# A four-layer cross-attention and feed-forward kernel: its first norm and query split made batch by batch, with queries moved to ScalarE's queue and selectors to GpSimd

## The chip, the core and the metric

The kernel runs on one core of a Trainium2 chip. The core has five engines, which run side by side and meet only at semaphores: TensorE (PE, matrix products), VectorE (DVE), ScalarE (ACT), GpSimd (POOL) and SyncE (SP), which here only issues DMA transfers. The metric is the device time of one execution in microseconds (us); lower is better.

## What is computed

The input `x` holds 2 batches of 256 tokens of width 128. Four layers follow, each a cross-attention or self-attention and a feed-forward block, each behind a norm. The change touches only the first attention, layer 0: 16 heads of width 8, queries from the normalised `x`, keys and values both the raw context of 2 batches of 512 tokens.

```python
def _layernorm(x, axis=-1, eps=1e-05):
    m = jnp.mean(x, axis=axis, keepdims=True)
    v = jnp.var(x, axis=axis, keepdims=True)
    return (x - m) / jnp.sqrt(v + eps)
...
        energy = jnp.einsum('nqhd,nkhd->nhqk', q, k)
        attn = jax.nn.softmax(energy / jnp.sqrt(jnp.float32(EMBED_SIZE)), axis=3)
        out = jnp.einsum('nhql,nlhd->nqhd', attn, v).reshape(N, q_len, EMBED_SIZE)
        return out @ w_out.T + b_out
...
    x = x + _L0_xattn_ref(ctx_1024, ctx_1024, _layernorm(x, axis=-1), L0_xattn_w_out, L0_xattn_b_out)
    x = x + _L0_ffn_ref(_layernorm(x, axis=-1), ...)
```

## The kernel before

The program is written engine by engine, with semaphores by hand; each engine works its own list in order, and an instruction that waits holds everything behind it on that engine. A DMA issue is an instruction of the engine whose queue it uses; before the change all of them are SyncE's.

**The first attention.** Scores are made in bf16, with each fp32 value split into three bf16 parts (`split_rows`, five VectorE steps: part 0, the rest, part 1, the rest, part 2). The parts of keys and queries lie with all heads in the partitions; the score products want one head's parts in rows. So they go through DRAM: `store_keys` and `store_queries` write the parts to `Kscr` and `Qscr`, `load_keys` and `load_queries` read them back into `Kst` and `Qst`, four heads per load, three loads per four heads. Rows 0 to 11 of `Kst` are *selectors*: ones that pick the right head's maximum out of rows 0 to 11 of `Qst`, where the split negative maximum of each query is written later. Before the change ScalarE writes all eight selector tiles (12x2048, four heads each).

**Groups and steps.** The 2 batches of 16 heads make 8 groups `g` of four heads; groups 0 to 3 are batch 0. `attention_cross(0)` runs in steps of 8 slots. In step `s`, TensorE makes the 8 maximum blocks of group `s` (`max_block`, L1761, one 128x512 product each, in two banks turn by turn, so that a block waits for the reduction two before it), and VectorE reduces each (`max_bank`, L993). GpSimd splits the group's maxima into three parts (`split_max`, L503 to L507), TensorE turns them in slot 4 of the next step (`turn_max`, L1818), and ScalarE copies them into `Qst` (L646). In step `s` TensorE also makes the scores of group `s - 2` (L1743), and the products of the exponentials with the values of group `s - 3` (L1845), which read `Vaug`, a copy of the context (L489, GpSimd). In the first three steps `max_block` is followed by busywork products (L1772), whose results nobody reads; `keep_busy` (L2060) is the same ahead of the attention.

**The opening, in the order of each list.** SyncE loads `x`, half of the turned context, the constants, the other half; then stores keys and queries of batch 0, with their loads mixed; then the context (`CTXN`), keys and queries of batch 1, and the weights. VectorE: statistics of all four tiles of `x`, the key split of batch 0, the norm of all four tiles, the query split of batch 0 (out of PSUM, after TensorE has turned the norm), the key and query splits of batch 1, the addition of the bias row `bo0` to `x`, and then the attention. GpSimd: the power of the variance (`rstd_of`), three casts, the wait for `CTXN` and its copy into `Vaug`, four memsets, and then `split_max` for all groups.

## Time and profile before

| | before |
|---|---|
| median of 3 runs | 552.3 us (551.53 to 555.41) |
| the profiled execution's own time | 551.78 us |
| its span, first to last instruction | 549.9 us |
| TensorE busy | 491.1 us (89%) |
| VectorE busy | 354.1 us (64%) |
| ScalarE busy | 309.8 us (56%) |
| GpSimd busy | 72.7 us (13%) |
| mean granted TensorE clock | 0.972 of full |

The span is one profiled execution. Busy times of different engines overlap, so they don't add up to it. An engine that is less than wholly busy is not free in every stretch; which engine sets the pace has to be read stretch by stretch. Products on TensorE are pipelined, so the duration of one contains its way through the array: the distance from one start to the next is what it costs in a row of them.

### The profile page before, as it was taken

Reading aid. Unit: us, or ns where it says so; the run is one execution under the profiler, and the core shown is the slowest. Engines: PE = TensorE matmul, PEld = TensorE weight load, DVE = VectorE, ACT = ScalarE, POOL = GpSimd, SP = SyncE. Lnnn points to the kernel's source line nnn. Section 1 sums busy time; section 2 is a strip of 40 time slices with the busy share of each in tenths; the row PEclk is TensorE's granted clock in tenths of the full one; section 3 lists DMA queues with packets and bytes.
Section 4 is the critical chain, followed back from the end, with each engine's and each line's share of the span. In section 5 each row is a group of like instructions: output and inputs, shape, how many; then the busy total and the mean of one; then the engine's idle time right before and its main releaser. Section 6 shows DMA issues by size and latency. Waiting matters only on the chain.

```text
span 549.9 us, 9205 instructions
## 1 busy us (share of the span) xinstructions
PE 491.1 (89%) x3320; PEld 302.8 (55%) x3324; DVE 354.1 (64%) x912; ACT 309.8 (56%) x530; POOL 72.7 (13%) x186
## 2 busy tenths in 40 slices
PE   5869998999989998798978599999999967898997
PEld 2224455998954444443734235555655655556987
DVE  5848755766689773398335647787698457545664
ACT  6428787463425779137366369888577404554331
POOL 4021111100011110000082000000042312000000
PEclk9979999999999999999999899999999977999999
DMA  4669401014425000000000000000000050000000
GB/s 144 189 167 400 166 2 36 1 30 131 123 63 176 3 0 2 1 1 0 2 0 0 2 0 0 1 2 1 2 1 2 15 217 0 1 1 2 2 10 11
DMA packets 11612, 26.17 MB, mean 48 GB/s; under 512 B 2128, under 2 KB 6864, under 8 KB 10928
## 3 DMA queue, kind: packets, MB, share of 16 engines
q1 hardware_dynamic: 11568, 25.59, 14.1%
q8 instruction: 27, 0.44, 0.4%
q14 instruction: 17, 0.14, 0.1%
HBM read 22.44 MB, written 3.15 MB: 47 GB/s over the span
## 4 chain that ended last, share of the span: by engine, by line
PE 71%; DVE 14%; issue 5%; ACT 5%; SPq 2%; DMA 2%; POOL 1%; DVEq 0%; ACTq 0%; POOLq 0%
PE ps L2091 5%; PE ps L2079 5%; PE ps L1761 5%; PE ps L1967 5%; PE ps L1978 5%; PE ps L1845 5%; PE ps L1993 5%; PE ps L1933 4%; PE ps L1743 4%; DVE mxs L993 3%; PE ps L2050 2%; PE ps L1945 2%; PE ps L1860 1%; PE ps L1772 1%; PE ps L2037 1%
## 5 line engine op out<-in xcount | busy, mean ns | idle before, releaser
L634 ACT ACTIVATE PR<-ps 128x1024 f32<-128x1024 f32 x80 | 77.4, 977 | 42.1 <-PE ps L1719 18.4
L993 DVE TENSOR_REDUCE mxs<-ps 128x1 f32<-128x512 f32 x128 | 81.7, 682 | 24.8 <-PE ps L1761 23.4
L1114 DVE TENSOR_REDUCE nm<-ps 128x1 f32<-128x512 f32 x64 | 41.1, 683 | 22.1 <-PE ps L1967 21.7
L1761 PE MATMUL ps<-Kst,Qst 84*128 84x512 bf16 x128 | 49.6, 394 | 6.2 <-DVE mxs L993 3.8
L678 ACT COPY PR<-ps 128x512 f32<-128x512 f32 x64 | 37.9, 595 | 21.9 <-PE ps L1978 21.9
L686 ACT ACTIVATE Qst<-ps,nm 128x512 f32<-128x512 f32 x64 | 45.5, 711 | 2.7 <-DVE nm L1114 2.7
L1743 PE MATMUL ps<-Qst,Kst 84*128 84x256 bf16 x256 | 46.1, 274 | 0.1
L468 POOL TENSOR_SCALAR ve<-mv 128x2 f32<-128x2 f32 (+1 forms) x13 | 3.0, 233 | 306.5 <-DVE mv L1171 169.3
L1978 PEld LDWEIGHTS ps<-const_t,Qst 128*128 128x128 f32 x256 | 27.5, 140 | 26.6 <-DVE Qst L1094 14.4
L717 ACT ACTIVATE PR<-ps,cols_t 128x256 f32<-128x256 f32 x64 | 26.5, 471 | 23.4 <-PE ps L2079 23.0
L1978 PE MATMUL ps<-const_t,Qst 128*128 128x128 f32 x256 | 35.4, 280 | 3.0 <-DVE Qst L1094 2.0
L1967 PE MATMUL ps<-VX,FC 64*128 64x512 f32 x128 | 36.1, 641 | 0.1
L1845 PE MATMUL ps<-PR,VX 128*9 128x256 f32 x512 | 33.5, 380 | 0.0
L646 ACT COPY Qst<-ps 12x1024 bf16<-12x1024 bf16 x20 | 20.0, 999 | 23.6 <-PE ps L1818 23.6
L1743 PEld LDWEIGHTS ps<-Qst,Kst 84*128 84x128 bf16 x256 | 23.5, 98 | 15.1 <-issue 3.4
L2091 PEld LDWEIGHTS ps<-FC,PR 128*128 128x128 f32 x256 | 30.9, 192 | 0.8
L1094 DVE TENSOR_SCALAR Qst<-Qst,rsum 128x512 f32<-128x512 f32 x64 | 30.6, 520 | 1.1
L2079 PE MATMUL ps<-parts,FC 128*128 128x256 f32 x128 | 30.4, 380 | 0.9 <-DVE scr L1054 0.8
L1993 PE MATMUL ps<-PR,Kst 128*64 128x256 f32 x256 | 31.2, 385 | 0.0
L1933 PE MATMUL ps<-scr,FC 128*128 128x256 f32 x128 | 30.6, 382 | 0.6 <-DVE scr L1054 0.6
L2091 PE MATMUL ps<-FC,PR 128*128 128x128 f32 x256 | 31.0, 275 | 0.0
L1761 PEld LDWEIGHTS ps<-Kst,Qst 84*128 84x128 bf16 x128 | 12.4, 98 | 32.9 <-DVE mxs L993 23.4
(389 smaller groups left out, 894.6 us busy)
## 6 DMA issues: line engine op xcount, KB each, us to landing
Kst<-k_rows SPq DMA_DIRECT2D x48, 96.0 KB
FC<-in_fc SPq DMA_DIRECT2D x2, 2048.0 KB, 12.2
Qst<-q_rows SPq DMA_DIRECT2D x48, 48.0 KB
FC<-in_w SPq DMA_DIRECT2D x1, 2048.0 KB, 7.4
k_rows<-REP SPq DMA_DIRECT2D x12, 128.0 KB, 2.2
REP<-in_w SPq DMA_DIRECT2D x1, 1536.0 KB, 7.2
q_rows<-REP SPq DMA_DIRECT2D x20, 64.0 KB, 2.0
FC<-in_w2e SPq DMA_DIRECT2D x1, 1024.0 KB, 9.4
```

The lines of the kernel that those rows point to most:

```text
L634: act.activation(PRg[:, g % 2, u * 1024:u * 1024 + width], bank(3 + 2 * (n % 2), 2)[:, 0:width], ACT.Exp, scale=scale).then_inc(s.p_ready, 1)
L686: act.activation(P3[:, i % 8, :], bank(S_BANKS[n % 2][half]), ACT.Exp, bias=nm3[:, i % 8:i % 8 + 1], accum_out=sum3[:, i % 16:i % 16 + 1]) ...
L993: i = dve.tensor_reduce(m[:, u // 4, u % 4:u % 4 + 1], bank(n % 2), AX_X, ALU.max)
L1743: i = pe.matmul(bank(3 + 2 * (n % 2), 2)[:, k * SQ:(k + 1) * SQ], Kst[0:ROWS_A, b, h0 + u, k * P:(k + 1) * P], Qst[0:ROWS_A, b, h0 + u, :] ...
L1761: pe.matmul(bank(n % 2), Qst[0:ROWS_A, b, h, q0:q0 + P], Kst[0:ROWS_A, b, h, :], start=True, stop=True).then_inc(s.smax_ready, 1)
L1845: i = pe.matmul(o[32 * c:32 * c + HD + 1, :], Vaug[:, 4 * b + k, h0 + c, 0:HD + 1], pr[:, c * 1024 + k * SQ:c * 1024 + (k + 1) * SQ], star ...
L1933: i = pe.matmul(bank(2 * (n % 2) + c // 2)[:, c % 2 * SQ:(c % 2 + 1) * SQ], w13[:, e, c * P:(c + 1) * P], lnT[:, b * SQ:(b + 1) * SQ], sta ...
L1967: pe.matmul(bank(S_BANKS[n % 2][half]), Q3[d0:d0 + DH3, r, q0:q0 + P], K3[d0:d0 + DH3, r, b * SK:(b + 1) * SK], start=True, stop=True)\
L1978: ins = pe.transpose(bank(T_BANKS[half])[:, k * P:(k + 1) * P], P3[:, i % 8, k * P:(k + 1) * P], ident)
L1993: pv = pe.matmul(bank(o3_bank(g))[DH3 * c:DH3 * (c + 1), r * SQ:(r + 1) * SQ], V3[:, 4 * b + k, DH3 * (h0 + 2 * r + c):DH3 * (h0 + 2 * r + ...
L2079: i = pe.matmul(bank(2 * (n % 2) + c // 2)[:, c % 2 * SQ:(c % 2 + 1) * SQ], fc1[:, n % E, c * P:(c + 1) * P], hdT[:, n % 3, :], start=True ...
L2091: i = pe.matmul(bank(4 + n % 2)[:, j * P:(j + 1) * P], actT[:, n % 2, c, j * P:(j + 1) * P], fc2[:, n % E, c, :], start=(c == 0), stop=(c ...
```

## The change

Five edits, all in the opening and in the first attention:

1. `x` is loaded in two halves, and statistics, power, norm and turn of norm 0 are done for each batch by itself. On VectorE the norm of batch 0 stands between the key split's second and third step; the statistics and norm of batch 1 follow after the queries of batch 0. TensorE's first two busywork products are gone and the eight behind become seven.
2. Batch 0's queries are stored and loaded from ScalarE's list, with batch 0's selectors between; SyncE issues all key loads of batch 0 without the queries between them.
3. Batch 1's four selectors are written by GpSimd, ahead of `split_max`.
4. GpSimd splits the maxima of groups 0 and 1 before it waits for the context and copies it. `CTXN` lies in another buffer (`scr` instead of `PR`). ScalarE no longer waits for that copy before the attention.
5. Batch 1's turned queries are copied by ScalarE from bank 7 to `lnT`, and VectorE splits them inside step 2, after its first reduction. The bias row `bo0` is added inside step 3.

```diff
-        CTXN = PR[:, 0:1024].rearrange("p (k n) -> p k n", k=KT)
+        CTXN = scr[:, T:3 * T].rearrange("p (k n) -> p k n", k=KT)
...
-            sp.dma_start(x[:, :, :], d["x"]).then_inc(s.ld_x, 16)
+            sp.dma_start(x[:, 0:2, :], d["x"][:, 0:2, :]).then_inc(s.ld_x, 16)
...
+            sp.dma_start(x[:, 2:4, :], d["x"][:, 2:4, :]).then_inc(s.ld_x1, 16)
             sp.dma_start(ctxT[:, SK:NK], d["ctxT"][:, SK:NK]).then_inc(s.ld_ctxT1, 16)
             store_keys(0, 0)
-            load_keys(0, 0, 0, 1)
-            store_queries(0, 0)
-            load_keys(0, 0, 1, 2)
-            load_queries(0, 0, 0, 2)
-            load_keys(0, 0, 2, 4)
-            load_queries(0, 0, 2, 4)
+            load_keys(0, 0, 0, 4)
             sp.dma_start(onesel[:, :, :], d["onesel"]).then_inc(s.ld_onesel, 16)
             sp.dma_start(CTXN, d["ctx"]).then_inc(s.ld_ctx, 16)
             store_keys(0, 1)
-            store_queries(0, 1)
+            store_queries(sp, 0, 1)
             load_keys(0, 1)
-            load_queries(0, 1)
+            load_queries(sp, 0, 1)
...
-            rstd_of(0)
+            for b in range(B):
+                rstd_of(0, b, of_batch(b))
...
-            pool.wait_ge(s.ld_ctx, 16)
-            pool.tensor_copy(Vaug[:, :, :, 0:HD], CTXN.rearrange("p k (h c) -> p k h c", h=H))\
-                .then_inc(s.setup_pool, 1)
-            link(pool.memset(onebv[:, :], 0.0))
-            for part in range(NPART):
-                link(pool.memset(onebv[32 * part:32 * part + 1, :], 1.0))
-            def split_max(a):
-
-                for g in range(G):
+            for q in range(4):
+                pool.tensor_copy(Kst[0:MAXR, 1, 4 * q:4 * q + 4, :],
+                                 C["selrow"][0:MAXR, 4 * q:4 * q + 4].unsqueeze(2).to_broadcast([MAXR, 4, SK]))\
+                    .then_inc(s.sel_ready1, 1)
+
+            def split_max(a, g0=0, g1=G):
+
+                for g in range(g0, g1):
...
-            split_max(0)
+            split_max(0, 0, 2)
+            pool.wait_ge(s.ld_ctx, 16)
+            pool.tensor_copy(Vaug[:, :, :, 0:HD], CTXN.rearrange("p k (h c) -> p k h c", h=H))\
+                .then_inc(s.setup_pool, 1)
+            split_max(0, 2, G)
+            link(pool.memset(onebv[:, :], 0.0))
...
-            for b in range(B):
-                for q in range(4):
-                    act.copy(Kst[0:MAXR, b, 4 * q:4 * q + 4, :],
-                             C["selrow"][0:MAXR, 4 * q:4 * q + 4].unsqueeze(2).to_broadcast([MAXR, 4, SK]))\
-                        .then_inc(s.sel_ready, 1)
-            act.wait_ge(s.setup_pool, 3)
...
+            select(0, 0)
+            select(0, 1)
+            store_queries(act, 0, 0)
+            load_queries(act, 0, 0, 0, 2)
+            select(0, 2)
+            load_queries(act, 0, 0, 2, 4)
+            select(0, 3)
+            act.wait_ge(s.xn_turned, 2)
+            act.copy(lnT[:, 0:SQ], bank(7)[:, 0:SQ]).then_inc(s.q0_copied, 1)
             attention(0)
...
+                        if a == 0 and step == 2 and part == 0:
+                            dve.wait_ge(s.q0_copied, 1)
+                            split_rows(Qparts[:, :, SQ:T], lnT[:, 0:SQ], rest[:, 0:SQ], None, 'q_split')
+                        if a == 0 and step == 3 and part == 0:
+                            add_row(C["bo0"])
...
+            turn_rows(0, 0, bank(0))
             pe.wait_ge(s.ld_ctxT, 16)
-            keep_busy(2, 7)
...
-            keep_busy(8, 6)
+            keep_busy(7, 6)
+            turn_rows(0, 1, bank(7))
```

How the lists change at the three places that matter here. In each row stands the source line, the operation, what it writes and reads, the size, and the semaphores for which it waits. SyncE before, from the keys of batch 0 to its last query load but one piece (L377 loads keys, L385 stores queries, L393 loads them):

```order
L377 DMA Kst<-k_rows 24x2048 [waits k_stored0]
L377 DMA Kst<-k_rows 24x2048 x2
L385 DMA q_rows<-REP 16x8x256 [waits q_split]
L385 DMA q_rows<-REP 16x8x256
L385 DMA q_rows<-REP 16x8x256 [waits q_split]
L385 DMA q_rows<-REP 16x8x256
L385 DMA q_rows<-REP 16x8x256 [waits q_split]
L377 DMA Kst<-k_rows 24x2048 [waits k_stored0]
L377 DMA Kst<-k_rows 24x2048 x2
L393 DMA Qst<-q_rows 24x1024 [waits q_stored0]
L393 DMA Qst<-q_rows 24x1024 x5
L377 DMA Kst<-k_rows 24x2048 [waits k_stored0]
```

ScalarE after, from its first selector to the attention (L707 selectors, L367 stores, L375 loads, L719 the copy of batch 1's queries):

```order
L707 CAST Kst<-const_t 12x2048 [waits ld_const]
L707 CAST Kst<-const_t 12x2048
L367 DMA q_rows<-REP 16x8x256 [waits q_split]
L367 DMA q_rows<-REP 16x8x256
L367 DMA q_rows<-REP 16x8x256 [waits q_split]
L367 DMA q_rows<-REP 16x8x256
L367 DMA q_rows<-REP 16x8x256 [waits q_split]
L375 DMA Qst<-q_rows 24x1024 [waits q_stored0]
L375 DMA Qst<-q_rows 24x1024 x5
L707 CAST Kst<-const_t 12x2048
L375 DMA Qst<-q_rows 24x1024 [waits q_stored0]
```

The stores and loads of batch 0's queries have left SyncE's list and stand in ScalarE's, between its selectors.

GpSimd before, from its power to the first split of maxima:

```order
L469 TENSOR_TENSOR rstd<-ve,nhalf 128x4 [waits pool_done]
L485 CAST identb<-const_t 128x128 [waits ld_const]
L486 CAST maskb<-const_t 128x128
L487 CAST maskb<-const_t 128x128
L489 COPY VX<-PR 128x128x8 [waits ld_ctx]
L491 MEMSET onebv 96x128
L493 MEMSET onebv 1x128 [waits pool_done] x3
L503 TENSOR_SCALAR mp<-mxs 128x2x4 [waits smax_read,pool_done]
```

And after (`VX` holds `Vaug`; L499 begins a group's split):

```order
L464 TENSOR_SCALAR ve<-mv 128x2 [waits var_ready]
L465 TENSOR_TENSOR rstd<-ve,nhalf 128x2 [waits pool_done]
L482 CAST identb<-const_t 128x128 [waits ld_const]
L483 CAST maskb<-const_t 128x128
L484 CAST maskb<-const_t 128x128
L486 CAST Kst<-const_t 12x2048 x4
L499 TENSOR_SCALAR mp<-mxs 128x2x4 [waits smax_read]
```

The wait for the context (`ld_ctx`) no longer stands ahead of the first split; four selectors and a second power do.

VectorE before, at the end of its opening:

```order
L970 CAST REP<-ps 128x256 [waits xn_turned,k_split]
L966 TENSOR_TENSOR rest<-ps,REP 128x256 [waits q_split]
L974 CAST REP<-rest 128x256 [waits dve_done]
L975 TENSOR_TENSOR rest<-rest,REP 128x256 [waits q_split]
L976 CAST REP<-rest 128x256 [waits dve_done]
L1138 TENSOR_TENSOR x<-x,const_t 128x512 [waits q_split]
L993 TENSOR_REDUCE mxs<-ps 128x1 [waits smax_ready,dve_done]
L993 TENSOR_REDUCE mxs<-ps 128x1 [waits smax_ready] x15
L993 TENSOR_REDUCE mxs<-ps 128x1 [waits smax_ready,m_ready]
```

And after, from the first reductions to step 3:

```order
L1005 TENSOR_REDUCE mxs<-ps 128x1 [waits smax_ready] x16
L1005 TENSOR_REDUCE mxs<-ps 128x1 [waits smax_ready,m_ready]
L982 CAST REP<-scr 128x256 [waits q0_copied]
L978 TENSOR_TENSOR rest<-scr,REP 128x256 [waits q_split]
L986 CAST REP<-rest 128x256 [waits dve_done]
L987 TENSOR_TENSOR rest<-rest,REP 128x256 [waits q_split]
L988 CAST REP<-rest 128x256 [waits dve_done]
L1005 TENSOR_REDUCE mxs<-ps 128x1 [waits smax_ready,q_split]
L1005 TENSOR_REDUCE mxs<-ps 128x1 [waits smax_ready] x6
L1005 TENSOR_REDUCE mxs<-ps 128x1 [waits smax_ready,m_ready]
L1155 TENSOR_TENSOR x<-x,const_t 128x512
```

The second batch's query split and the bias row have moved behind 17 and 25 reductions.

## Rows read from the trace of the kernel before

**Rows 1.** The page: the span, and busy time of TensorE

```profile
span 549.9 us, 9205 instructions
PE 491.1 (89%) x3320; PEld 302.8 (55%) x3324; DVE 354.1 (64%) x912; ACT 309.8 (56%) x530; POOL 72.7 (13%) x186
```

**Rows 2.** The chain that ended last, 26 to 44: start us, us, what

```profile
23.25 5.24 DMA PR<-in_ctx
28.55 1.04 POOL VX L489
...
30.58 0.27 POOL mp L503
...
32.10 0.38 PE ps L1818 x2
```

**Rows 3.** TensorE's timeline: start us, busy us, line, operation, tiles, shapes, count

```profile
5.76 3.78 PE L2060 MATMUL ps<-ctxT,const_t 128*128 128x512 f32 x4 [5.76 <-DMA const_t<-in_const]
...
10.19 7.47 PE L2060 MATMUL ps<-ctxT,const_t 128*128 128x512 f32 x16
18.71 0.59 PE L1761 MATMUL ps<-Kst,Qst 84*128 84x512 bf16 x2 [1.05 <-DMA Qst<-q_rows]
...
26.70 0.38 PE L1761 MATMUL ps<-Kst,Qst 84*128 84x512 bf16 x1
...
42.82 0.38 PE L1761 MATMUL ps<-Kst,Qst 84*128 84x512 bf16 x1
...
49.62 0.39 PE L1761 MATMUL ps<-Kst,Qst 84*128 84x512 bf16 x1
```

**Rows 4.** Stretches: us, busy of PE, PEld, DVE, ACT, POOL; PEclk; DMA; GB/s

```profile
27.00:32.10 5.10, 0.08 (x1) 0.00 (x0) 0.69 (x1) 0.00 (x0) 2.90 (x10) 0.95 0.58 172
32.10:38.30 6.20, 6.20 (x17) 2.34 (x18) 3.22 (x5) 1.00 (x1) 1.10 (x5) 0.50 0.75 186
```

**Rows 5.** SyncE's timeline, its DMA issues: key loads, query stores, query loads

```profile
10.93 3.10 SPq L385 DMA_DIRECT2D q_rows<-REP  x5
...
15.49 2.41 SPq L393 DMA_DIRECT2D Qst<-q_rows  x6
...
29.58 4.80 SPq L377 DMA_DIRECT2D Kst<-k_rows  x12
```

**Rows 6.** ScalarE's timeline: the eight selectors

```profile
5.74 14.48 ACT L704 CAST Kst<-const_t 12x2048 bf16<-12x2048 f32 x8 [3.53 <-DMA const_t<-in_const]
```

**Rows 7.** VectorE's timeline: keys' first step, norm, query split, bias row

```profile
4.70 0.39 DVE L970 CAST REP<-ctxT 128x512 bf16<-128x512 f32 x1
...
7.50 1.20 DVE L878 TENSOR_SCALAR xn<-x,mv,rstd 128x128 f32<-128x128 f32 x4
10.43 0.42 DVE L970 CAST REP<-ps 128x256 bf16<-128x256 f32 x1 [1.74 <-PE ps L2067]
...
12.14 0.29 DVE L976 CAST REP<-rest 128x256 bf16<-128x256 f32 x1
...
17.33 0.69 DVE L1138 TENSOR_TENSOR x<-x,const_t 128x512 f32<-128x512 f32 x1
```

**Rows 8.** Query stores (L385), whole span: from issue to landing

```profile
DMA to landing us min/median/max: 1.9/2.0/2.6
```

**Rows 9.** GpSimd's groups by shape: busy us, mean ns of one, idle before

```profile
L469 POOL TENSOR_TENSOR rstd<-ve,nhalf 128x2 f32<-128x2 f32 x8 | 5.8, 720 | 0.7
...
L489 POOL COPY VX<-PR 128x1024 f32<-128x1024 f32 x1 | 1.0, 1042 | 20.7 <-DMA PR<-in_ctx 20.7
...
L546 POOL CAST parts<-rest 128x320 bf16<-128x320 f32 x1 | 0.5, 526 | 0.1
L486 POOL CAST maskb<-const_t 128x128 bf16<-128x128 f32 x1 | 0.5, 513 | 0.0
...
L544 POOL CAST parts<-rest 128x320 bf16<-128x320 f32 x1 | 0.5, 451 | 0.1
...
L487 POOL CAST maskb<-const_t 128x128 bf16<-128x128 f32 x1 | 0.3, 293 | 0.0
```

More of the change, by code:

```diff
@@ L278, in mega_kernel @@
         NUNIT = B * E
-        NORMS = [(0, 0), (1, 0), (2, 0), (1, 1), (2, 1), (3, 0), (3, 1)] + [(k, 0) for k in range(4, 8)] + \
+        NORMS = [(0, 0), (0, 1), (1, 0), (2, 0), (1, 1), (2, 1), (3, 0), (3, 1)] + [(k, 0) for k in range(4, 8)] + \
             [(8, 0), (9, 0), (8, 1), (9, 1), (10, 0), (10, 1)]
@@ L360, in group_heads, with store_queries, load_queries @@
             return g // 4, 4 * (g % 4)
+        def store_queries(queue, phase, b):
+            for i in range(NPART):
+                queue.wait_ge(s.q_split, NPART * (2 * phase + b) + i + 1)
+                for at in ((i, i + NPART) if i < 2 else (i,)):
+                    queue.dma_start(Qscr[b, HD * at:HD * (at + 1), :, :].rearrange("c h k -> h c k"),
+                                 Qparts[:, i, b * SQ:(b + 1) * SQ]).then_inc(S[f"q_stored{b}"], 16)
+        def load_queries(queue, phase, b, q0=0, q1=4):
+            queue.wait_ge(S[f"q_stored{b}"], 16 * (NPART + 2) * (phase + 1))
+            for q in range(q0, q1):
+                for a in range(NPART):
+                    queue.dma_start(Qst[MAXR + PROWS * a:MAXR + PROWS * (a + 1), b, 4 * q:4 * q + 4, :],
+                                 Qscr[b, HD * a:HD * a + PROWS, 4 * q:4 * q + 4, :])\
+                        .then_inc(S[f"q_loaded{b}{q}"], 16)
         @block.sync
@@ L508, in split_max @@
                     pool.wait_ge(s.m_ready, groups(a, g) + 1)
-            split_max(0)
+            split_max(0, 0, 2)
[4 more added lines that the diff above has]
+            link(pool.memset(onebv[:, :], 0.0))
+            for part in range(NPART):
+                link(pool.memset(onebv[32 * part:32 * part + 1, :], 1.0))
             for b in range(B):
@@ L1231, in _ @@
             dve.wait_ge(s.ld_x, 16)
[L1232 removed]
+            batch_variances(0)
             dve.wait_ge(s.ld_ctxT, 16)
[L1234 to L1243 removed]
+            keys = ctxT[:, 0:SK]
+            signal(dve.tensor_copy(Kparts[:, 0, 0:SK], keys), 'k_split')
+            link(dve.tensor_tensor(rest[:, 0:SK], keys, Kparts[:, 0, 0:SK], ALU.subtract))
+            batch_normalised(0, 0)
+            signal(dve.tensor_copy(Kparts[:, 1, 0:SK], rest[:, 0:SK]), 'k_split')
+            link(dve.tensor_tensor(rest[:, 0:SK], rest[:, 0:SK], Kparts[:, 1, 0:SK], ALU.subtract))
+            signal(dve.tensor_copy(Kparts[:, 2, 0:SK], rest[:, 0:SK]), 'k_split')
+            dve.wait_ge(s.xn_turned, 1)
+            split_rows(Qparts[:, :, 0:SQ], bank(0)[:, 0:SQ], rest[:, 0:SQ], None, 'q_split')
+            dve.wait_ge(s.ld_x1, 16)
+            batch_variances(1)
+            dve.wait_ge(s.ld_ctxT1, 16)
+            split_rows(Kparts[:, :, SK:NK], ctxT[:, SK:NK], rest[:, 0:SK], None, 'k_split')
+            batch_normalised(0, 1)
             attention(0)
@@ L1791, in attention_cross @@
                             queries1(1, bank(5))
+                        if a == 0 and step == 2 and slot == 0:
+                            pe.wait_ge(s.q0_copied, 1)
                         if a == 1 and step == 2 and slot == 0:
@@ L2046, in values3 @@
                         pe.wait_ge(s.bv_ready, 2)
-                        pe.wait_ge(s.rstd_ready, 2)
+                        pe.wait_ge(s.rstd_ready, norm(1) + 1)
                     if n >= 3:
```

44 lines of the change are left out of this document (10 added, 34 removed).

## The prediction

> **What bounds the kernel now.** The page is read first: TensorE is busy for 89% of a 549.9 us span, so a stretch in which it stands still is worth looking for [rows 1]. The chain of work that ended last, followed through the opening, finds one. From 23.25 us it does not run through TensorE: it goes from the load of the context, landed 5.24 us after its issue, to GpSimd's copy of it (28.55), through GpSimd's memsets and the splitting of the first maxima, to TensorE's turn of these at 32.10 [rows 2]. The first 13 maximum blocks had gone out from 18.71 to 26.70, one each 7.99 / 12 = 0.666 us [rows 3]. GpSimd could have split the maxima of group 0 after eight of them, but its program puts the copy of the context first.
>
> The table by stretches tells the price. From 27.0 to 32.1 TensorE works 0.08 us; then, to 38.3, it works without a gap at a granted clock of 0.50, the lower of its two levels, 1.2 against 2.4 GHz [rows 4]. Before it fell, TensorE had been idle for five microseconds.
>
> The prediction follows four marks on TensorE, L1761's blocks: the first at 18.71, the thirteenth at 26.70, step 3's first at 42.82 and step 4's first at 49.62 [rows 3]. From step 4 on no instruction order changes; whatever step 4 gains should reach the end.
>
> **Part 1, queries from ScalarE's queue.** Before, SyncE issues query stores at 10.93 (five in 3.10), three key loads, and query loads from 15.49, six in 2.41 or 0.40 each [rows 5]. The third load, at 16.3, fills the first group; TensorE starts at 18.71, 2.4 after it. ScalarE is held by eight selectors from 5.74 to 20.2, 1.81 each [rows 6]. After, it makes two (to 9.4) and then issues the stores. VectorE's last query part was ready at 12.43; now two normalisations of 0.30 instead of four stand ahead of it, and its transposes no longer queue behind TensorE's two busywork products, which ended at 9.54 [rows 3, 7]. Five key steps took 2.8 (4.70 to the norm at 7.50) and two normalisations take 0.6, which gives about 8.2; the half microsecond that shorter statistics save is lost again to waiting for GpSimd's power (`rstd_of`). A query split takes 2.0 (10.43 to 12.43): ready at 10.2 [rows 7]. The stores thus hang on ScalarE: 9.4 + 3.1 = 12.5 with SyncE's price per issue; the last is issued at 11.9 and lands 2.0 later [rows 8], at 13.9. Loads go out then, the third at 14.7, and 2.4 on is 17.1. No ScalarE issue is in the trace; its bounds are nothing and SyncE's 0.62, and I take the latter, the same instruction. With nothing, the last part lands at 12.2 and TensorE could start at 14.6, when its own opening is not through (below), so 16.3 is the early bound. I add 0.4 for key loads in flight at the same time, since landing ranges up to 2.6 instead of 2.0 [rows 8]: start at **17.5**, 1.2 earlier; bounds 16.3 and 18.7.
>
> TensorE's opening is shorter: two transposes and seven products, then two transposes. A product was two instructions of 0.945 in the first stretch and 0.467 later (3.78 / 4, 7.47 / 16) [rows 3]. Starting at 7.4, with the rate turning after five to seven instructions, fourteen end at 16.3 to 17.3; the start stays as above. If it did not turn, they would end at 20.6.
>
> **Part 2, GpSimd.** It gains a second small norm, behind VectorE's second variance (11.0): 0.3 and 0.72, then three casts of 0.29 to 0.51 [rows 9], so at 13.4 it starts four selectors of 12x2048. No row has that operation on GpSimd. Copying 1024 elements took 1.04 us, 1.02 ns an element; casts of 128 and 320 elements took 0.29 and 0.45, and a line through them gives 0.82 ns an element and 1.87 for 2048 [rows 9]. I take 2.0 each, so the four end at 21.4. The bounds are 1.7 (that slope alone) and 8.2 (sixteen times the slowest short cast, 0.513 [rows 9]).
>
> Now the maxima of groups 0 and 1 are split before the context is waited for. Group 0's eight reductions are done at 17.5 + 5.8 = 23.3; GpSimd's five steps take about 1.5 (from 30.58 to 32.10 in the chain) [rows 2], so they are there at 24.8. TensorE reaches the turn after thirteen blocks, at 17.5 + 8.2 = 25.7. The idle five microseconds and the low clock behind them are gone. The selectors have cover until 23.3, 1.9 us; up to 24.2, 2.7 us each, TensorE still doesn't wait.
>
> The copy of the context moves behind group 1's maxima, about 30.3, and ends at 31.3. Its reader is the first product with values, in the middle of step 3, at about 38: hidden by 6 us.
>
> **Part 3, what VectorE takes over inside the attention.** The second batch's split (2.0) and the bias row (0.69) lay before the first maximum [rows 7]. They now stand between maximum reductions, in steps 2 and 3. VectorE sets the pace there: 0.666 a block means 5.35 for a step of eight. TensorE can go only two blocks ahead, so it waits behind the split: step 2 costs 5.35 + 2.0 + 0.35 for turn and product work out of phase = 7.7 (bounds 5.5 and 8.0). Step 3 took 6.80 and has some reduction idleness behind its products with values; of the 0.69 I charge half: 7.15 (6.80 to 7.49).
>
> **The sum.** Start 17.5, sixteen blocks 10.65 -> 28.15, step 2 -> 35.85, step 3 -> 43.0, against 49.62: 6.6 less. By pieces, with 1.2 from the start, this says that the stall and low clock gave back 8.1 and the moved VectorE work took 2.7. The profiled execution is at 551.78, 0.52 below the median, 552.3. 551.78 - 6.6 = 545.2 in its terms, and **545.7** as a median.
>
> **What costs nothing, and its cover.** SyncE now waits in step 2 for the second split, until 31.6. Queued behind: five stores, twelve key loads, twelve query loads and all weights. Stores start with the first part at 30.0 and take 3.1; twelve key loads take 4.80 [rows 5], twelve query loads as long. The first three query loads go out from 37.9 and land at 41.1. Step 4 needs them at 43.0: cover 1.9 us; anything beyond it is paid in full. The weights follow at about 42.7, some 3 us later than now, and the first is wanted at step 8, near 70. The ScalarE copy of the second batch's turned queries is ready by 22.9 (two selectors, twelve loads), wanted at 29.5. Half loads of x and the changed place of the context (nothing else uses it until step 4) cost nothing.
>
> **Rivals.** *The selectors are somewhat late.* A 320-element cast also took 0.526 us, 1.64 ns an element [rows 9]: 3.4 each, ending at 26.9, maxima split at 28.4, and TensorE waits 2.7. The gain falls to 3.9: 548.4. For it: the same operation; against: the slope of 0.82 ns. The Trainium skill (GPSIMD Engine Reference, "3.1 Elementwise — side-by-side cycle accounting") gives about 1.8 cycles an element at 1.2 GHz for a tight loop; as an estimate from that page, 3.1 us each, ending at 25.8, a wait of 1.6 and 547.3. No row has this length; the copy at 1.02 ns an element speaks against it.
>
> *The other side: slower.* The selectors are as slow as the 0.513 cast: 8.2 each, done at 46.2, split at 47.7. TensorE would stand for 22 us and then run at half rate for six, some 2 us more: 551.78 + 22 + 2 - 6.6, about 569. It decides from 3.9 us each: then the wait (4.8) and the low clock (2.1, the half rate over six blocks: 6.2 against 4.1) eat the 6.6. For it: only the short casts, of which the third took 0.29.
>
> *The queries land no sooner.* Before, the 16 transfer engines had no other key load in flight behind a query store; now twelve key loads go out from 10.5 without a pause. If that gives back the 1.2, the gain is 5.4: 546.9. A query load later than 18.7 gives back one for one. The Trainium skill (DMA: Bandwidth & Descriptors, "Issuing engines are not separate DMA queues") says that issuing from several engines saves issue time alone, as all share the transfer engines. The trace shows issue times (0.40 and 0.62) that were indeed in the way; two queues at once it doesn't show.
>
> **How the numbers follow.** Forecast 0.66; selectors somewhat late 0.14; queries no sooner 0.13; slower 0.07. The forecast's own range runs from 543.5 (start 16.3 and half of the split hidden: 6.6 + 1.2 + 1.0 = 8.8 less) to 547.5 (step 3 dearer, opening later). The range over the cases, **543.3 to 549.0**, leaves out the slow selectors and some 0.06 on either side. This kernel's measurement can tell about 1% from no change, 5.5 us: faster means below 546.8. Three quarters and more of the forecast (0.53), a part of the late queries (0.05) and a little of the selectors (0.01) lie there: 0.59. Slower is the fourth case and a little more: 0.08. The rest, 0.33, is within 1%.
>
> **What would show it.** On TensorE's rows: first block near 17.5, no wait of microseconds at the first turn (GpSimd's five steps ending ahead of 25.7), no stretch at 0.50 in the first 45 us, step 2 about 7.7 long with a VectorE split inside, step 4 near 43.0, and the same distance from there to the end. GpSimd's selector rows near 2.0 each. It is wrong if the selectors take over 2.7, if the clock falls during the 2 us wait in step 2, if the second batch's query load arrives after 43.0, or if step 4's gain is lost behind it.

## The result, and the profile after

| | before | after |
|---|---|---|
| median of 20 runs each | 553.27 us (547.31 to 555.41) | 558.4 us (551.68 to 567.31) |
| ratio after / before | | 1.007 [1.0046, 1.0094] |
| the profiled execution's own time | 551.78 us | 560.81 us |
| its span | 549.9 us | 558.8 us |
| mean granted TensorE clock in it | 0.972 | 0.954 |

The change makes the kernel slower, by 5.1 us in the medians and by 0.7% in the ratio. The ratio leaves out the five of the changed kernel's twenty executions that lie more than 1.5% above its fastest (without them its median is 556.48, 3.2 us above the kernel before); the one profiled is among the five, so its rows show where the loss comes from rather than its usual size.

The page of after begins as follows (busy time, share of the span, instructions; then the granted clock in 40 slices; then the DMA queues). TensorE's busy time is 6.0 us more than in [rows 1], though the change leaves out three of its products:

```profile
span 558.8 us, 9203 instructions
PE 497.1 (89%) x3318; PEld 304.4 (54%) x3318; DVE 357.1 (64%) x912; ACT 303.5 (54%) x527; POOL 82.0 (15%) x192
PEclk9786999999988999999999879999999987999999
q10 hardware_dynamic: 1152, 0.92, 0.5%
```

Queue q10 is ScalarE's, new. The clock's digits show the first thing that was not forecast: 7, 8 and 6 in the second to fourth slice, a slice being 14 us.

TensorE's timeline of after (start, duration, operation, count; in brackets the idle time ahead and what ended it). L2083 is the busywork, L1641 the turn of the norm, L1782 the maximum blocks, L1841 the first turn of split maxima; these rows answer to [rows 3] and to the last row of [rows 2]:

```profile
7.44 7.41 PE L2083 MATMUL ps<-ctxT,const_t 128*128 128x512 f32 x14
16.25 0.44 PE L1641 MATMUL ps<-const_t,xn 128*128 128x128 f32 x2 [1.40 <-DVE xn L1195]
21.11 1.01 PE L1782 MATMUL ps<-Kst,Qst 84*128 84x512 bf16 x2 [4.41 <-DMA Qst<-q_rows]
...
31.44 0.28 PE L1841 MATMUL ps<-identb,mp 128*12 128x128 bf16 x2
...
38.23 0.61 PE L1782 MATMUL ps<-Kst,Qst 84*128 84x512 bf16 x1 [2.46 <-DVE mxs L1005]
...
54.45 0.39 PE L1782 MATMUL ps<-Kst,Qst 84*128 84x512 bf16 x1
```

The first block comes at 21.11, not at 17.5. The wait at the first turn is gone: the row at 31.44 has no bracket, where before there were 5 us. A new wait of 2.46 us stands in step 2 behind VectorE, and step 4's first block comes at 54.45: 4.8 us later than before, where 6.6 earlier was forecast.

Three stretches of the same trace (from and to, length; busy time and instructions of TensorE, its weight loads, VectorE, ScalarE and GpSimd; then the granted clock, the share of busy transfer engines and GB/s):

```profile
14.85:21.10 6.25, 0.44 (x2) 0.23 (x3) 1.35 (x1) 1.90 (x1) 6.25 (x4) 0.92 0.83 230
20.40:27.20 6.80, 6.09 (x15) 2.20 (x16) 3.78 (x6) 2.16 (x2) 1.23 (x1) 0.52 0.44 156
37.50:51.10 13.60, 12.83 (x52) 5.11 (x52) 8.00 (x12) 6.00 (x6) 1.10 (x5) 0.51 0.73 187
```

From 14.85 to 21.1 TensorE works 0.44 us; then the clock is at its lower level, 1.2 GHz, to 27.2. Behind the wait in step 2 it is there again, from 37.5 to 51.1. Before, there was one such stretch in the opening, behind one wait [rows 4]; now there are two, and the second is twice as long.

Why the first block is late is in the chain of waits of after (start, duration, what held):

```profile
11.45 3.89 DMA q_rows<-REP
...
16.35 4.52 DMA Qst<-q_rows
```

The last query store, issued at 11.45 (forecast 11.9), took 3.89 us to land instead of 2.0 [rows 8], and the load that TensorE waits for took 4.52. The rows of the two queues (SPq is SyncE's, ACTq is ScalarE's; L394 are key loads, L367 query stores, L375 query loads) show what else was under way:

```profile
10.64 5.39 SPq L394 DMA_DIRECT2D Kst<-k_rows  x12
8.85 3.21 ACTq L367 DMA_DIRECT2D q_rows<-REP  x5
15.37 2.83 ACTq L375 DMA_DIRECT2D Qst<-q_rows  x6
```

All twelve key loads go out between 10.64 and 16.0, around the last stores and ahead of the awaited load (16.35). The share of busy transfer engines from 14.85 to 21.1 is 0.83.

Two more rows, of VectorE and GpSimd at the same time, show something that was not in the forecast at all. VectorE's two normalisations of 0.30 take 2.28 beside the first of GpSimd's selectors; the selectors themselves took 7.41 / 4 = 1.85 each:

```profile
13.92 2.28 DVE L1195 TENSOR_SCALAR xn<-x,mv,rstd 128x128 f32<-128x128 f32 x2
14.23 7.41 POOL L486 CAST Kst<-const_t 12x2048 bf16<-12x2048 f32 x4
```

### The profile page after: what moved, and what is told of

Same layout as the page of the kernel before. It is cut to its first block, busy times and chain, and to the rows that moved or that the text cites. A ratio compares the mean times of both kernels' runs of the same rounds, so it can differ in the third digit from the quotient of the medians.

```text
span 558.8 us, 9203 instructions
## 1 busy us (share of the span) xinstructions
PE 497.1 (89%) x3318; PEld 304.4 (54%) x3318; DVE 357.1 (64%) x912; ACT 303.5 (54%) x527; POOL 82.0 (15%) x192
## 4 chain that ended last, share of the span: by engine, by line
PE 73%; DVE 14%; issue 5%; ACT 4%; DMA 2%; POOL 1%; ACTq 0%; DVEq 0%; POOLq 0%
PE ps L1782 6%; PE ps L2111 5%; PE ps L2099 5%; PE ps L1990 5%; PE ps L1868 5%; PE ps L2001 5%; PE ps L2016 5%; PE ps L1764 4%; PE ps L1956 4%; DVE mxs L1005 3%; PE ps L1793 3%; PE ps L2073 2%; PE ps L1968 2%; PE ps L2258 2%; PE ps L1883 1%
## 5 line engine op out<-in xcount | busy, mean ns | idle before, releaser
L1782 PE MATMUL ps<-Kst,Qst 84*128 84x512 bf16 x128 | 52.8, 424 | 11.5 <-DVE mxs L1005 5.5
L1764 PE MATMUL ps<-Qst,Kst 84*128 84x256 bf16 x256 | 48.0, 283 | 0.1
L1782 PEld LDWEIGHTS ps<-Kst,Qst 84*128 84x128 bf16 x128 | 13.0, 103 | 37.9 <-DVE mxs L1005 24.4
```

What stands on the lines that cost most here:

```text
L1764: i = pe.matmul(bank(3 + 2 * (n % 2), 2)[:, k * SQ:(k + 1) * SQ], Kst[0:ROWS_A, b, h0 + u, k * P:(k + 1) * P], Qst[0:ROWS_A, b, h0 + u, :] ...
L1782: pe.matmul(bank(n % 2), Qst[0:ROWS_A, b, h, q0:q0 + P], Kst[0:ROWS_A, b, h, :], start=True, stop=True).then_inc(s.smax_ready, 1)
```

## The experiments

A ratio is always to the kernel before, run beside it on the same chip.

**1. GpSimd's order alone** (the kernel before with edit 4 only):

```diff
...
-            pool.wait_ge(s.ld_ctx, 16)
-            pool.tensor_copy(Vaug[:, :, :, 0:HD], CTXN.rearrange("p k (h c) -> p k h c", h=H))\
-                .then_inc(s.setup_pool, 1)
...
-            split_max(0)
+            split_max(0, 0, 2)
+            pool.wait_ge(s.ld_ctx, 16)
+            pool.tensor_copy(Vaug[:, :, :, 0:HD], CTXN.rearrange("p k (h c) -> p k h c", h=H))\
+                .then_inc(s.setup_pool, 1)
+            split_max(0, 2, G)
...
```

> The kernel before with edit 4 alone: GpSimd splits the maxima of groups 0 and 1 before it waits for the context, whose buffer and ScalarE's wait change with it; queries stay on SyncE, selectors on ScalarE, both query splits in the opening. Theory (the edit that removes the 5 us wait is good, and the others lose its gain): first block at 18.7 as before, no wait at the first turn, no stretch at 0.50 near 32 to 38, step 4's first block near 42 (18.7 + 10.65 + 5.4 + 6.8 = 41.6) instead of 49.6, and 7 to 8 us less, ratio 0.985 to 0.988. Rival (the wait only moves: something else holds step 2 or 3 to its old time, or the low clock comes anyway): step 4 at 47 or later, ratio 0.995 or more.

Measured: 0.9934 [0.9907, 0.9961], 547.94 us; profiled span 543.0. TensorE's timeline (L1761 the blocks, L1818 the turn, as before):

```profile
18.86 0.59 PE L1761 MATMUL ps<-Kst,Qst 84*128 84x512 bf16 x2 [2.00 <-DMA Qst<-q_rows]
...
28.22 0.28 PE L1818 MATMUL ps<-identb,mp 128*12 128x128 bf16 x2
...
42.99 0.39 PE L1761 MATMUL ps<-Kst,Qst 84*128 84x512 bf16 x1
```

The turn has no wait, and step 4's first block comes 6.6 us earlier than in [rows 3]. So the first half of the argument holds, on its own: the wait for the context was the price, and this edit alone takes it away. The ratio and the medians give 3.6 to 4.2 us of it, less than the 6.6 at step 4 (experiments 8 and 9). The clock does fall in the opening here, to 0.57 from 20.2 to 23.6, behind the wait of 2.00 for the queries.

**2. The second batch's split back in the opening** (the change without edit 5):

```diff
...
             batch_normalised(0, 1)
+            dve.wait_ge(s.xn_turned, 2)
+            split_rows(Qparts[:, :, SQ:T], bank(7)[:, 0:SQ], rest[:, 0:SQ], None, 'q_split')
+            add_row(C["bo0"])
             attention(0)
```

> The changed kernel with edit 5 undone: batch 1's query split and the bias row stand ahead of the first reduction again, where VectorE of the changed kernel idled from 16.2 to 21.7. Theory (the 2.5 us wait in step 2 is the split's, and it pulls the clock down for 13.7 us behind it): no wait in step 2, no low clock from 38 to 51, step 4's first block 8 to 9 us sooner than in the changed kernel (54.5), near 46; ratio to the kernel before 0.990 to 0.996. Rival (the second low stretch belongs to the late start and comes anyway): step 4 only 2 us sooner, ratio 1.00 to 1.005.

Measured: 0.9996 [0.9971, 1.0021], 552.16 us. The blocks start as late as in the change, the wait in step 2 is gone, and the only low clock of the opening is that behind the start (0.52 from 22 to 28):

```profile
21.13 1.01 PE L1778 MATMUL ps<-Kst,Qst 84*128 84x512 bf16 x2 [4.38 <-DMA Qst<-q_rows]
...
46.85 0.39 PE L1778 MATMUL ps<-Kst,Qst 84*128 84x512 bf16 x1
```

Step 4 begins 7.6 us earlier than in the change's profiled execution. In the ratio edit 5 is worth 1.007 against 0.9996: it costs 0.7%.

**3. The key loads behind the first queries** (the change, with SyncE holding nine of its twelve key loads until the first group's queries have landed):

```diff
-            load_keys(0, 0, 0, 4)
+            load_keys(0, 0, 0, 1)
+            sp.wait_ge(s.q_loaded00, 16 * NPART)
+            load_keys(0, 0, 1, 4)
```

> The changed kernel, but SyncE issues only the first three key loads of batch 0 and waits until the first group's queries have landed before the other nine. Theory (nine key loads in flight on the same transfer engines hold back ScalarE's query stores, 3.9 us to land instead of 2.0, and its first loads, 4.5 instead of 2.4): stores land in about 2.1, first block near 17.5 instead of 21.1, no low clock from 21 to 27. Rival (ScalarE's queue lands later by itself, whatever else is in flight): first block stays near 21.

Measured: 0.9966 [0.9937, 0.9995], 551.13 us. TensorE's rows:

```profile
17.04 0.59 PE L1784 MATMUL ps<-Kst,Qst 84*128 84x512 bf16 x2 [0.52 <-DMA Qst<-q_rows]
...
32.05 0.39 PE L1784 MATMUL ps<-Kst,Qst 84*128 84x512 bf16 x1 [2.46 <-DVE mxs L1007]
...
43.38 0.39 PE L1784 MATMUL ps<-Kst,Qst 84*128 84x512 bf16 x1
```

The first block comes at 17.04, 4.1 us earlier than in the change: the transfers in flight had held the queries back. The wait holds back more than nine key loads: also what stands behind them on SyncE's list, the constants `onesel`, the context (512 KB, issued at 16.48 in the change) and the second batch's key stores. The store's 3.89 us in the change ended before any of these was issued, so those are the key loads'; in the load's 4.52 us the two aren't told apart. In this execution the clock did not fall behind the wait of 2.46, and step 4 begins at 43.38 where the prediction had 43.0. Yet the span is 548.6, only 1.3 shorter than before: 5 us of the gain were lost behind step 4.

**4. Both of these** (experiments 2 and 3 together).

> The changed kernel with both edits of the two kernels ahead of it: split and bias row back in the opening, nine key loads behind the first queries. Theory: first block near 17.5, no stretch at 0.50 in the opening, step 4 near 41 and 8 to 9 us less than before, ratio 0.983 to 0.987, so better than edit 4 alone by a microsecond. Rival (GpSimd's selectors and VectorE stand in each other's way, as VectorE's two normalisations at 13.9 took 2.28 instead of 0.60 and one cast in step 2 1.01 instead of 0.29): start at 18.7 or later, and no better than edit 4 alone.

Measured: 0.9994 [0.9973, 1.0015], 552.13 us, not the sum of the two. The first block comes at 17.26, but the second pair waits for VectorE until 23.51:

```profile
17.26 0.59 PE L1780 MATMUL ps<-Kst,Qst 84*128 84x512 bf16 x2 [0.59 <-DVE REP L982]
23.51 1.21 PE L1780 MATMUL ps<-Kst,Qst 84*128 84x512 bf16 x2 [5.00 <-DVE mxs L1005]
```

VectorE's rows of the same trace show why: two steps of the split take 1.99 and 1.86 us, where the same steps took 0.43 and 0.29 for the first batch (at 9.62 and 10.09 in this trace). GpSimd's four selectors run from 14.21 to 21.85:

```profile
17.16 0.42 DVE L978 TENSOR_TENSOR rest<-ps,REP 128x256 f32<-128x256 f32 x1
17.62 0.46 DVE L986 CAST REP<-rest 128x256 bf16<-128x256 f32 x1
18.11 1.99 DVE L987 TENSOR_TENSOR rest<-rest,REP 128x256 f32<-128x256 f32 x1
20.13 1.86 DVE L988 CAST REP<-rest 128x256 bf16<-128x256 f32 x1
...
22.76 2.68 DVE L1005 TENSOR_REDUCE mxs<-ps 128x1 f32<-128x512 f32 x4
```

**5. The same with all selectors on ScalarE** (experiment 4 with edit 3 undone too):

```diff
-            for q in range(4):
-                pool.tensor_copy(Kst[0:MAXR, 1, 4 * q:4 * q + 4, :],
-                                 C["selrow"][0:MAXR, 4 * q:4 * q + 4].unsqueeze(2).to_broadcast([MAXR, 4, SK]))\
-                    .then_inc(s.sel_ready1, 1)
...
             select(0, 3)
+            for q in range(4):
+                select(1, q)
...
```

> The change with the second batch's query split and the bias row back in the opening, the key loads behind the first queries, and now also the second batch's four selectors written by ScalarE again, behind its own four. Theory: GpSimd's selectors slow VectorE's work at the same time. In the kernel without this last edit two steps of the split took 1.99 and 1.86 us, where the same steps took 0.43 and 0.29 before GpSimd began, and the first reductions came at 22.76. Without GpSimd's selectors the split takes 2.1 us from about 16.7, the bias row ends near 19.5, the reductions start there, 3.3 us earlier, and step 4's first block comes at 42.5 to 44 instead of 47.47; ratio to the kernel before 0.985 to 0.994. Rival: VectorE is late because it waits for the turn of the second norm, or because PSUM is read by others; then the split's rows stay near 2 us and step 4's block stays near 47.

Measured: 0.9921 [0.989, 0.9953], 548.66 us. The split is back at its old price and the reductions start at 18.06 instead of 22.76:

```profile
16.55 0.43 DVE L984 TENSOR_TENSOR rest<-rest,REP 128x256 f32<-128x256 f32 x1
17.01 0.29 DVE L985 CAST REP<-rest 128x256 bf16<-128x256 f32 x1
...
18.06 2.48 DVE L1002 TENSOR_REDUCE mxs<-ps 128x1 f32<-128x512 f32 x4
```

TensorE's row of step 4:

```profile
41.64 0.39 PE L1777 MATMUL ps<-Kst,Qst 84*128 84x512 bf16 x1
```

Step 4's first block comes at 41.64, 8.0 us earlier than before and 5.8 earlier than in experiment 4 (where the clock was at 0.52 from 23.5 to 29.7, behind the wait of 5.00), and the trace has no low clock in the first 200 us. Moving the selectors to GpSimd is what slowed VectorE. The selectors on ScalarE have a price too: they end at 28.56, and TensorE's first scores wait 0.92 us for ScalarE's copy of the turned maxima. This kernel and that of experiment 1 beat both the kernel before and the change; their intervals overlap, so neither is shown to be the better.

**6. Work for TensorE in the two gaps of the change**:

```diff
             turn_rows(0, 1, bank(7))
+            keep_busy(4, 6)
...
-                            for _ in range(3 if step < 2 else 2):
+                            for _ in range(3 if step < 2 else 11 if a == 0 and slot == 1 else 2):
```

> The change with work for TensorE in its two gaps, whose result nobody reads: four products more ahead of the first block, nine short ones more behind the second block of step 2. Theory: the low clock behind the two gaps is what the changed kernel loses against the one before; the gaps themselves stay. First block near 21.1 as in the change, step 2 still waits for VectorE's split, but no stretch at 0.50 in the first 50 us: step 4's first block at 46 to 48 instead of 54.45, ratio to the kernel before 0.990 to 0.997 (the change: 1.007). Rival: the clock falls whatever TensorE does between, or what follows pays it back by a low stretch later: step 4 still near 54, or step 4 earlier and the end not; ratio 1.002 to 1.010.

Measured: 1.0018 [0.9992, 1.0044], 553.28 us. The gaps' ends stay (first block at 21.63), filled with products that nobody reads, and the clock stays up:

```profile
16.54 3.60 PE L2083 MATMUL ps<-ctxT,const_t 128*128 128x512 f32 x8
21.63 0.59 PE L1782 MATMUL ps<-Kst,Qst 84*128 84x512 bf16 x2 [1.49 <-DMA Qst<-q_rows]
...
32.93 2.54 PE L1793 MATMUL ps<-REP,identb 128*128 128x512 bf16 x11
...
47.97 0.39 PE L1782 MATMUL ps<-Kst,Qst 84*128 84x512 bf16 x1
```

Two stretches of it, that behind the start and that behind the split:

```profile
17.00:27.00 10.00, 8.11 (x29) 2.84 (x27) 4.80 (x8) 4.05 (x3) 4.63 (x3) 1.00 0.70 191
32.70:46.00 13.30, 11.90 (x79) 5.65 (x79) 11.75 (x20) 7.64 (x8) 4.14 (x11) 1.00 0.51 133
```

Step 4's first block comes at 47.97, 6.5 earlier than in the change's profiled execution, with nothing made faster but the clock. Against the kernel before, the ratio of 1.007 [1.0046, 1.0094] becomes 1.0018, no longer told from 1; in the medians, 1.3 us (552.0 to 553.28) are left of 3.2. The ratio lies above the range that was expected: step 4 is 1.6 earlier than before, the end is not (experiments 8 and 9).

**7. The queries back on SyncE's queue** (the change with edit 2 undone; the order of SyncE's issues as before, and ScalarE issues nothing).

> The change with its queue edit undone: the first batch's queries are stored and loaded by SyncE between the key loads, in the order of the kernel before; ScalarE writes its four selectors without transfers between. Theory: what delays the first block in the change is the twelve key loads in flight, not the queue that issues the queries. Then the first block comes at 17.5 to 18.7 instead of 21.11, because only three key loads are ahead of the query stores again, and the ratio to the kernel before falls below the change's 1.007, to 0.994 to 1.002. Rival: the query parts themselves come too late from VectorE (the norm by halves does not bring them forward): then the first block stays at 20 or later.

Measured: 1.0121 [1.0077, 1.0164], 560.19 us from six runs. SyncE's queue and TensorE's first block:

```profile
10.70 1.16 SPq L394 DMA_DIRECT2D Kst<-k_rows  x3
11.89 3.10 SPq L367 DMA_DIRECT2D q_rows<-REP  x5
...
16.45 2.41 SPq L375 DMA_DIRECT2D Qst<-q_rows  x6
...
19.65 1.01 PE L1784 MATMUL ps<-Kst,Qst 84*128 84x512 bf16 x2 [2.88 <-DMA Qst<-q_rows]
```

The first block comes 1.5 us earlier than in the change, so beside all twelve key loads ScalarE's queue made it worse; but 0.9 later than before: SyncE's first query store is issued at 11.89, 10.93 in [rows 5], behind key loads that start only at 10.70, since the key split now has a norm in it. Beside experiment 3 (17.04) it shows what ScalarE's queue is worth once no bulk of key loads is in its way: 2.6 us at the first block. The last store is issued at 14.40, there at 11.28: on SyncE's list the stores stand behind three key loads, and these behind the landing of the key stores (10.68). The three key loads behind the stores cost nothing: they are issued by 16.40, and the last store lands at 16.42. The median went the other way than expected; the interval of the ratio overlaps the change's, so neither is shown to be the slower. Four of its six executions lie at 560.2 to 560.6 with a mean clock of 0.954, two near 555 with 0.960 and 0.963, the profiled one among them; this kernel has the wait in step 2 as the change has it, but what the four did there was not profiled. So why an earlier start brought no better time stays open.

**8 and 9. The kernel before, held at its start** by one or two extra loads ahead of the first real one; nothing else is changed.

```diff
+            for i in range(1):
+                sp.dma_start(rest[:, :].rearrange("p (t n) -> p t n", t=NT), d["x"]).then_inc(s.held, 16)
+                sp.wait_ge(s.held, 16 * (i + 1))
             sp.dma_start(x[:, :, :], d["x"]).then_inc(s.ld_x, 16)
```

> The kernel before, held once at its start: SyncE loads the input into a buffer that is free then and waits for it, before its first real load. Nothing else is changed. It asks what a bare shift of the whole program does, since in the kernel with keys late and selectors on ScalarE 8.0 us were won up to 300 us and 2.7 lost again by 320. If the later stages cost the same wherever they fall in time: first block 2.0 to 2.6 later (20.7 to 21.3), every later mark as much, ratio 1.004 to 1.005. If the places where the clock falls hang on the time at which a stage comes: stretches at 0.50 stand at other places of the program than in the kernel before, and the end moves by 2.3 plus or minus up to 4 us, ratio 0.997 to 1.012.

> The kernel before, held twice in the same way. If the later stages cost the same wherever they fall: first block 4.0 to 5.2 later, every later mark as much, ratio 1.008 to 1.009. If the clock's low stretches move against the program: the end moves by 4.6 plus or minus up to 4 us, and the difference to the kernel held once is not 2.3.

Measured: 1.0053 [1.0018, 1.0088] and 1.0124 [1.0041, 1.0207]; the medians are 2.4 and 5.8 us longer. The first block comes 2.7 and 5.0 later. Each interval reaches into both of the ranges that were named for it, so the ratios don't decide between them. The marks speak against the first reading, by which every later mark is as late as the first block: held once, the wait at the first turn shortens (3.33 instead of 5.03), and the first product of layer 0's feed-forward part, at 90.70 before, is only 0.6 late; held twice, 4.3. The spans are 3.4 and 6.8 longer. So from that product to the end the same program took 2.8 and 2.5 us longer. That this is because it came at another time isn't shown: these are single executions, and those of the kernel before, not held, lie 8 us apart (547.31 to 555.41). That part of the program, from this product to the end, as one stretch of each of six kernels: before, the change, experiments 1, 5, 3 and 8 (columns as above):

```profile
90.70:549.90 459.20, 414.48 (x2773) 268.35 (x2776) 296.42 (x790) 251.26 (x470) 52.92 (x123) 0.97 0.08 25
95.50:558.80 463.30, 418.50 (x2776) 270.00 (x2776) 296.81 (x790) 251.49 (x470) 52.95 (x123) 0.97 0.08 25
84.10:543.00 458.90, 413.79 (x2776) 266.80 (x2776) 296.92 (x790) 250.79 (x470) 52.62 (x123) 0.98 0.08 25
82.70:545.40 462.70, 418.95 (x2776) 270.40 (x2776) 296.75 (x790) 251.24 (x470) 52.79 (x123) 0.97 0.08 25
84.50:548.60 464.10, 420.37 (x2776) 270.68 (x2776) 296.78 (x790) 251.44 (x470) 52.96 (x123) 0.96 0.08 25
91.30:553.30 462.00, 417.10 (x2776) 269.16 (x2776) 296.72 (x790) 251.44 (x470) 52.95 (x123) 0.97 0.08 25
```

VectorE, ScalarE and GpSimd work as long in all six, within 0.7 us; TensorE, with the same instructions, from 413.79 to 420.37. What differs is for how much of it the clock was low. One place where it shows is the same part of the program around 300 us, in the kernel of experiment 5 and in the kernel before:

```profile
282.00:318.00 36.00, 27.45 (x86) 13.10 (x85) 19.81 (x59) 17.42 (x29) 3.77 (x6) 0.81 0.00 1
290.10:323.40 33.30, 23.85 (x84) 11.42 (x85) 19.80 (x59) 17.27 (x29) 3.77 (x6) 0.90 0.00 1
```

With the clock at 0.81 instead of 0.90, 2.7 us of the 8.0 that were won are lost here. Why the clock falls there once and not another time isn't settled: the instructions are the same.

**10. The split in step 2, with the start mended** (experiment 5, but with edit 5 left in):

> The change with the key loads behind the first queries and the second batch's selectors on ScalarE, but with the second query split and the bias row left inside the attention, as the change has them: against the kernel with the split back in the opening only that edit differs. Theory: VectorE sets the pace of the first steps, so work moved from in front of its reductions into them is not saved. First block near 17.4 and first reduction near 17.9, hardly ahead of 18.06, since the blocks wait for the queries; the split then stands in step 2, where TensorE waits 2.4 us for it, and step 4's first block comes at 43.2 to 43.6 instead of 41.64. Where the clock falls behind that wait, it comes later still. Ratio to the kernel before 0.994 to 1.002, against 0.9921. Rival: moving it is worth its 2.7 us, since the reductions start earlier by as much: step 4's first block at or before 41.6, ratio 0.988 to 0.992.

Measured: 0.9956 [0.9924, 0.9987], 551.4 us (546.81 to 557.99; experiment 5: 545.89 to 550.12). The first reduction comes at 17.46, 0.6 before that of experiment 5, not 2.7: the blocks wait for the queries. The split then stands in step 2. TensorE waits there 1.61 us for ScalarE's copy of the turned maxima, which stands behind the selectors, and 0.78 for VectorE, where 2.4 for VectorE were expected. Behind these waits the clock falls in the profiled execution (TensorE's row, and the stretch):

```profile
29.61 0.38 PE L1763 MATMUL ps<-Qst,Kst 84*128 84x256 bf16 x2 [1.61 <-ACT Qst L646]
```

```profile
31.80:38.60 6.80, 6.54 (x21) 2.77 (x22) 3.92 (x7) 3.04 (x4) 0.00 (x0) 0.51 0.63 174
```

Step 4's first block comes at 46.44 instead of 41.64. Without the low clock, as an estimate from experiment 3, it would have come near 43.4, so at this mark the edit loses either way, by 1.8 or by 4.8. The intervals of the two ratios overlap; their order is that of the marks.

## Why the prediction was wrong, by its steps

**Right.** The wait at the first turn and its cause, GpSimd's order: gone, and in experiment 1 worth 6.6 us at step 4. The sum gave this edit 8.1; that its total for the whole change is 6.6 too is chance. GpSimd's selectors: 1.85 us against 2.0, done at 21.6 against 21.4. The query parts: ready at 10.4 against 10.2. The last store: issued at 11.45 against 11.9, though not held by ScalarE's selectors as the prediction has it (the first store is issued at 8.85, while the second selector runs to 9.46), but by VectorE's last part. Where the start was mended and the clock held, in experiment 3, the marks came near the forecast: first block 17.04 against 17.5, step 4 at 43.38 against 43.0. The steps between took 26.34 us against 25.5: step 2 took 8.25 and step 3 7.53, just beyond their bounds of 8.0 and 7.49. In step 2 GpSimd's copy of the context, which edit 4 puts beside the split, goes with a last cast of 1.01 instead of 0.29. TensorE's busywork ended even sooner than forecast, at 14.85.

**The step that failed first: "I add 0.4 for key loads in flight".** It should have been 4.0: 17.1 became 21.11. The term was sized from landings of 1.9 to 2.6 us in [rows 8]; batch 0's among them had three key loads issued ahead and three behind, not none, as the prediction says of the latter. With twelve the store took 3.89 (1.9 more) and the awaited load 4.52 (2.4 more with the start behind it), and experiment 3 turns 21.11 into 17.04 by holding nine loads back, and with them the context and the key stores behind them. The rival that the queries land no sooner had the right cause, but priced it at the 1.2 us that could be won; of what lies beyond, it says only that a later load gives back one for one, without a size. The Trainium skill (DMA: Bandwidth & Descriptors, "Issuing engines are not separate DMA queues") says that transfers of several engines share the 16 transfer engines and interleave; the trace agrees (3.89 us for the store instead of 2.0). Its further statement is that a second issuing engine saves only issue time, usually little beside the transfer. Here it was not little: between experiments 7 and 3 the last store's issue differs by 3.1 us, SyncE's order included, beside a landing of 2.02 and 2.68.

**The second: "The idle five microseconds and the low clock behind them are gone", hence "no stretch at 0.50 in the first 45 us".** The forecast took away one idle stretch of TensorE and the low clock behind it. It did not ask what the change puts in. Two idle stretches came, the 6.25 us ahead of the first block (where edit 1 also takes three busywork products out) and the 2.46 in step 2, and the clock fell behind both. The prediction named the second as what would make it wrong, "if the clock falls during the 2 us wait in step 2", but gave it no chance and no price. Experiment 6 gives the price of both together: from the first block to step 4 it takes 26.34 us instead of 33.34, and the ratio is 1.0018 instead of 1.007. Experiment 2 gives that of edit 5, 0.7%. Behind the wait of 2.46 the clock fell in the profiled execution of the change and did not in those of experiments 3 and 7, where the wait is as long. Nor does the length of a wait decide elsewhere: the clock fell behind 2.00 us (experiment 1, first block) and not behind 2.22 (experiment 5, first block). The widths of the ranges of times (551.68 to 567.31 for the change, 549.9 to 555.46 for experiment 2) fit that it falls in some executions only.

**The third: GpSimd's selectors cost VectorE nothing.** "The selectors have cover until 23.3" looked at who waits for the selectors by a semaphore. VectorE does not, and was slowed all the same: 2.28 for two normalisations of 0.30, and in experiment 4 a delay of 3.1 us in the split, which experiment 5 takes away by moving the selectors alone. In the change this price at the start is hidden, since VectorE has time until 21.7; it appears once the queries come sooner. The Trainium skill (SBUF — State Buffer, "Who interferes with whom") says that VectorE and GpSimd share one pair of ports, that it is locked for a whole instruction, and that `tensor_tensor` with two inputs in SBUF, casts and `tensor_scalar` can want it while `tensor_reduce` does not. The rows agree: the slowed steps are of these kinds; those of the split are longer by 1.6 us each, somewhat less than one selector of 1.85 to 1.91; the step of 17.16, with one input in PSUM, took its usual 0.42, and four reductions beside the selectors in experiment 3 (17.45) their usual 2.48. A cast at 17.62, at 0.46 instead of 0.29, was hardly slowed; why is open.

**The fourth: "whatever step 4 gains should reach the end".** Of 6.2 to 8.0 us at step 4, experiments 3 and 5 had 1.3 and 4.5 left at the end of their profiled executions, and their medians show 0.3% and 0.8%. Behind 90 us, where the instructions are the same, single executions of the twelve kernels took from 458.9 to 464.2 us, and experiments 8 and 9 took 2.5 to 2.8 longer than the kernel before with nothing changed but a held start. The kernel before was profiled at 459.2, near the lower end, so what step 4 gains against it overstates what is won at the end. The difference lies in how long the clock is low there; why it falls at one place in one kernel and at another in the next stays open.

**Edit 5 in itself** was charged with what it moves, 2.7 us inside the steps. The start gained 0.6 of it in experiment 10, since the blocks wait for queries, not for VectorE. So moving 2.7 us into the stretch where VectorE sets the pace was a loss before any clock: 43.38 at step 4 in experiment 3, against 41.64 in experiment 5 (whose selectors stand elsewhere, too).

**The time.** Forecast 545.7 in 543.3 to 549.0; measured 558.4. In the profiled execution step 4 is 11.4 us later than forecast (54.45 against 43.0): 3.6 from the start, 7.0 from the two stretches of low clock (33.34 us from the first block to step 4, against 26.34 in experiments 3 and 6) and 0.8 from steps dearer than forecast (26.34 against 25.5). The tail adds 4.1 against the profiled execution of before. The forecast gave slower 0.08; the one mechanism it priced for it, selectors of 8.2 us, did not occur, and the one that did occur it had named without a price.

## What to carry to other kernels

A transfer that starts the work of the whole program should not share the transfer engines with bulk loads that are needed later: hold these back by a semaphore, and size their effect by how many are in flight, not by the landing times of a quieter stretch. Before moving work to an idle engine or into a later stretch, list the new idle times that it gives TensorE and price the clock behind each, and ask which engine shares a port with the one that gets the work. Measure a kernel of this kind by medians over many runs: the same instructions behind 90 us took up to 5 us more in one profiled execution than in another.

## What the runs showed of the hardware

- VectorE beside a running GpSimd cast: 0.43 became 1.99, 0.29 became 1.86, two of 0.30 became 2.28; beside GpSimd's copy of 1.20 us at 36.09 in the change, a cast of 0.29 took 1.01.
- ScalarE issues transfers while its own cast runs: in the change its first query store is issued at 8.85, its second selector ends at 9.46. A store's issue took 0.61 us there, about that of SyncE (0.60).
